# Attention and gated MLP, post-norm: normalisation scratch kept across head pairs, and four PSUM banks instead of two in the output projection

## What is computed

```python
q, k, v = x @ Wq, x @ Wk, x @ Wv                  # 16 heads of 64
s   = einsum(q, k) / 8 - 50 * strictly_upper      # per head, 2048 x 2048
att = softmax(s) @ v                              # heads joined: 1024 wide
y1  = layernorm(x + att @ Wr)
# every product below takes an int8-like row of activations and ternary weights:
#   aq(a) = clip(round(a * 127 / max|a|), -128, 127) * max|a| / 127
#   wq(w) = clip(round(w / mean|w|), -1, 1) * mean|w|
h   = silu(aq(y1) @ wq(w_gate).T) * (aq(y1) @ wq(w_up).T)
out = layernorm(y1 + aq(h) @ wq(w_down).T)
```

## Time and profile before

| | us |
|---|---|
| runs shown, median (lowest to highest) of 2 | 7385.25 (7290.29 to 7480.22) |
| the profiled execution | 7288.75 |
| its span on the slowest core (core 2) | 7287.2 |
| spans of the eight cores | 7242.9 to 7287.2 |
| attention of sequence 1 (pairs 1 to 8), from the first projection matmul | 164 to 2378 |
| attention of sequence 2 | 3961 to 5867 |
| output projection, sequence 1 and 2 | 2419 to 2607 and 5905 to 6092 |

### The profile page before, as it was taken

The page is one execution under the profiler, slowest core; times in us unless marked ns, Lnnn a source line. Parts: engine busy times, 40 slices in busy tenths (PEclk is TensorE's granted clock), DMA queues, the critical chain, the costliest instruction groups (busy, mean ns, idle before and its releaser), DMA issues.

```text
span 7287.2 us, 56300 instructions; the slowest of 8 cores (7242.9 to 7287.2 us)
## 1 busy us (share of the span) xinstructions
PE 5021.0 (69%) x17593; PEld 1861.4 (26%) x17938; DVE 2901.0 (40%) x4986; ACT 1127.3 (15%) x2132; POOL 0.2 (0%) x4
## 2 busy tenths in 40 slices
PE   0777777767778775674732877888888877576474
PEld 0222222222222232231310222222222223232131
DVE  1545455455454432321302444444444443232231
ACT  0112112112112011110100211221122211011010
POOL 0000000000000000000000000000000000000000
PEclk9888878877888888897976888998899988898887
DMA  4324233233231445445453000000000044545454
GB/s 104 93 78 105 62 105 98 65 87 107 62 87 34 134 132 145 132 150 150 133 169 71 14 18 18 12 14 18 18 16 11 10 118 127 143 131 171 129 150 141
DMA packets 803555, 649.78 MB, mean 89 GB/s; under 512 B 518336, under 2 KB 715200, under 8 KB 803264
## 3 DMA queue, kind: packets, MB, share of 16 engines
q1 hardware_dynamic: 803264, 646.16, 32.8%
HBM read 469.89 MB, written 75.50 MB: 75 GB/s over the span
## 4 chain that ended last, share of the span: by engine, by line
PE 54%; DMA 19%; DVE 15%; issue 6%; ACT 4%; SPq 1%; DVEq 0%; ACTq 0%
PE bank L160 53%; DMA wdsb<-wdT_sc 7%; ACT abuf L171 3%; DVE rls L209 3%; DMA hqT<-hq 3%; DMA XT_lo<-xlo 1%; DMA XT_hi<-xhi 1%; DMA pterT<-pter 1%; DMA pw<-Wd 1%; DVE pacc L204 1%; DVE apwl L193 1%; DVE vp L198 1%; DMA XqT<-xqtm 1%; DMA x_tm<-x 1%; PE bank L166 1%
## 5 line engine op out<-in xcount | busy, mean ns | idle before, releaser
L171 ACT ACTIVATE abuf<-bank,negC 128x512 f32<-128x512 f32 (+3 forms) x1664 | 833.3, 601 | 3061.6 <-DVE bank L188 2139.1
L160 PE MATMUL bank<-abuf,vp 128*65 128x512 f32 x2560 | 1253.9, 649 | 0.0
L160 PE MATMUL bank<-wdsb,hqT 128*128 128x512 bf16 x2008 | 539.2, 417 | 676.8 <-DMA wdsb<-wdT_sc 674.8
L160 PE MATMUL bank<-XT_hi,apwh 128*128 128x512 bf16 x1444 | 435.8, 457 | 688.2 <-DVE apwl L193 678.9
L209 DVE RECIPROCAL rls<-bank 1x512 f32<-1x512 f32 x128 | 429.4, 3355 | 705.9 <-PE bank L160 705.4
L160 PE MATMUL bank<-klp,khl 128*128 128x512 bf16 x1184 | 467.8, 395 | 325.2 <-ACT abuf L171 317.6
L160 PE MATMUL bank<-wgsb,XqT 128*128 128x512 bf16 x2010 | 493.6, 387 | 238.6 <-DMA wgsb<-wgT_sc 234.0
L160 PEld LDWEIGHTS bank<-abuf,vp 128*65 128x65 f32 x2560 | 375.8, 151 | 838.3 <-issue 838.2
L160 PE MATMUL bank<-qlo,khp 128*128 128x512 bf16 x1280 | 511.2, 399 | 27.5 <-DVE vp L198 20.0
L160 PE MATMUL bank<-wusb,XqT 128*128 128x512 bf16 x2004 | 483.2, 381 | 4.3 <-DMA wusb<-wuT_sc 2.0
L160 PEld LDWEIGHTS bank<-wdsb,hqT 128*128 128x128 bf16 x2048 | 201.4, 105 | 1013.7 <-issue 859.8
(11 more groups left out here) (90 smaller groups left out, 3346.4 us busy)
## 6 DMA issues: line engine op xcount, KB each, us to landing
wdsb<-wdT_sc SPq DMA_DIRECT2D x256, 512.0 KB, 4.0
wgsb<-wgT_sc SPq DMA_DIRECT2D x64, 1024.0 KB, 7.7
wusb<-wuT_sc SPq DMA_DIRECT2D x64, 1024.0 KB, 10.1
pw<-Wg SPq DMA_DIRECT2D x64, 512.0 KB, 4.4
pw<-Wu SPq DMA_DIRECT2D x64, 512.0 KB, 4.3
pw<-Wd SPq DMA_DIRECT2D x64, 512.0 KB, 5.0
x_tm<-x SPq DMA_DIRECT2D x8, 2048.0 KB, 18.1
xrd<-x SPq DMA_DIRECT2D x32, 512.0 KB, 5.2
```

The lines of the kernel that those rows point to most:

```text
L160: e.matmul(o, l, r, start=a, stop=b),
L171: e.activation(o, i, f, bias=b, scale=s, accum_out=a),
```

## The change

The scratch tiles of the normalisation are allocated once per sequence, in `run_seq`, and handed to `attn_pair`. The flush at the end of every pair goes; it is now called once per sequence, after the eighth pair (`flush_norm`). The closures of a pair's last block are thus called in the first block of the next pair, where before nothing was pending: `do_norm_pre`, `pump_prep(3)`, and after that block's scores `do_normalize` with `pump_prep(4)`. `avslot` is set to 1 at the head of the blocks of each pair, so a pair's eighth block always uses bank 4, which the next pair's projections into banks 0 to 3 and its transposes don't touch. In `wr_ln1` odd chunks use banks 6 and 7 instead of 4 and 5.

```diff
@@ run_seq
+            _al0 = lambda *a, **k: _es0.enter_context(self.sbg(*a, **k)).ap()
+            nbufs = (_al0("rls", [128, 512], F32),
+                     _al0("rlb", [128, 1024], BF16),
+                     _al0("osr", [64, 512], F32),
+                     _al0("onf", [64, 512], F32),
+                     [_al0("ogh0", [64, 512], BF16),
+                      _al0("ogh1", [64, 512], BF16)],
+                     [_al0("ogl0", [64, 512], BF16),
+                      _al0("ogl1", [64, 512], BF16)])
...
                     for pair in range(c.PAIRS):
-                        self.attn_pair(s, pair, XT_hi, XT_lo, wstage)
+                        self.attn_pair(s, pair, XT_hi, XT_lo, wstage, nbufs)
+                    self.flush_norm()
                     self.pump_prep(10 ** 6)
             else:
                 for pair in range(c.PAIRS):
-                    self.attn_pair(s, pair, XT_hi, XT_lo, wstage)
+                    self.attn_pair(s, pair, XT_hi, XT_lo, wstage, nbufs)
+                self.flush_norm()
+    def flush_norm(self):
+        if self.norm_pending is not None:
+            self.norm_pending[0]()
+            self.norm_pending[1]()
+            self.norm_pending = None
@@ attn_pair
-            rls = al("rls", [128, 512], F32)
...
+            rls, rlb, osr, onf, ogh, ogl = nbufs
+            self.avslot = 1
             t_ot_last = None
             for h in (0, 1):
@@ attn_pair, after the blocks
-            if self.norm_pending is not None:
-                self.norm_pending[0]()
-                self.norm_pending[1]()
-                self.norm_pending = None
@@ wr_ln1, in the matmul loop and again in the loop that empties the banks
-                            bk = 4 + jt
+                            bk = 4 + 2 * (tc % 2) + jt
```

More of the change, by code:

```diff
@@ L490, in prefetch_w, with attn_pair @@
                 src, waits=self.wsplit_toks[name])
-    def attn_pair(self, s, pair, XT_hi, XT_lo, wstage):
+    def attn_pair(self, s, pair, XT_hi, XT_lo, wstage, nbufs):
         c = self.c
```

## The result

The changed kernel is faster: the ratio to the kernel before is 0.979, 95% interval 0.973 to 0.985, so that it is not decided whether the gain is more than 2%. The profiled executions took 7149.67 (after) and 7288.75 us (before). The forecast was 7166, a ratio of 0.983. Over all runs the medians are 7333.82 (11 runs, 7114.46 to 7489.85) and 7484.58 (10 runs, 7287.15 to 7738.39); in many executions of either kernel the cores of a die, sometimes of both, were granted a lower clock and the run was some per cent longer, and the ratio is taken from the others.

What follows compares the result with a forecast made beforehand. PE, holding 54% of the span, sets the pace, so its waits count. Output projection -41, seams -53 and -46, steps +17 sum to -123, from 7288.75 to 7166 us; range 7118 to 7265.

Steps and rivals of the forecast that it cites:

- the output projection: Part 1, wr_ln1: banks 6 and 7 for odd chunks remove a 1.38 us bank wait per chunk; -41 us.
- something else takes over: Rival, also called The output projection: it is held by something else, half of the 41 us gone; 7186 us, chance 0.07.
- the seam: Between pairs, without preparation: -10.7 stop, -1.8 clock, +5.0 first block; -53 us in second sequence, -46 in first.
- the clock's 1.8 in the Q projection: Q projection after a seam: full clock without a stop before it, -1.8 us per seam in the second sequence.
- part 3: Pumped preparation steps of the first sequence: leaving the seams, partly for the first blocks, costs +17 us together.
- stops at a new weight, met elsewhere: First sequence's seams: 19 us fell where a new weight begins without its loads, and would be met elsewhere.
- The twins: A pair's fifth and sixth blocks, used to price steps in its first (+3.2 us) and second (+4.9 us).
- The first sequence gains nothing: Rival: short pumped blocks stall another 4.1 us per seam, so sequence 1's 29 us are gone; 7195 us, chance 0.14.
- Better: Rival: steps hide at seams as well as elsewhere (-17), first block gives back 3.9, not 5.0 (-15); 7134 us, chance 0.17.
- The clock: Rival: closing PE's gaps on all eight cores brings the granted clock down; 7356 us, 0.9% above before, chance 0.10.
- a clock between its levels: Sign in the profile after that would show the forecast wrong: a granted clock between the levels 1.0 and 0.5.

Runs made afterwards that it cites:

- the run with steps at the seam again: Changed kernel, no steps in a pair's first block, four at its end ahead of next weight split; first attention stage 2181 us (cores 0 to 5).

## Why the prediction was right or wrong

**Right: the output projection.** -41.0 against -41, with chunks at 10.36 for 10.37, the clock at 1.00 and the DMA share at 0.52 for 0.51. The rival that something else takes over is out.

**Right, by sums that nearly cancel: the seam.** Without steps, seven seams went from 72.3 to -1.1, 10.5 each for my 10.7; seven first blocks from 52.3 to 89.0, +5.2 each for +5.0. Of the clock's 1.8 in the Q projection less came. That projection does start at full clock, but TensorE is at half clock for longer in the rest of the pair. Windows over one pair of the second sequence, in equal parts of the pair, before and then after (columns as the earlier trace rows):

```profile
4682.30:4706.30 24.00, 22.39 (x94) 9.61 (x94) 4.20 (x7) 0.00 (x0) 0.00 (x0) 0.92 0.07 22
4706.30:4747.30 41.00, 26.95 (x105) 11.53 (x109) 24.17 (x32) 0.00 (x0) 0.00 (x0) 0.83 0.12 33
4747.30:4789.30 42.00, 34.10 (x129) 14.14 (x129) 14.76 (x48) 5.63 (x11) 0.00 (x0) 0.88 0.08 19
```

```profile
4555.80:4579.80 24.00, 20.92 (x97) 9.29 (x95) 5.65 (x9) 0.00 (x0) 0.00 (x0) 1.00 0.00 0
4579.80:4620.80 41.00, 29.00 (x109) 11.84 (x110) 22.72 (x30) 0.00 (x0) 0.00 (x0) 0.76 0.12 32
4620.80:4662.80 42.00, 33.18 (x117) 13.43 (x116) 16.91 (x51) 2.99 (x7) 0.00 (x0) 0.75 0.09 22
```

0.92 became 1.00, and 0.83 and 0.88 became 0.76 and 0.75. The third window takes in the first block, and what falls there is that block's clock. First and second block of the same pair, before and then after:

```profile
4777.02:4784.19 7.17, 7.17 (x16) 2.32 (x16) 1.20 (x4) 3.20 (x7) 0.00 (x0) 0.69 0.00 0
4784.19:4800.27 16.08, 13.63 (x35) 3.96 (x35) 7.92 (x11) 5.30 (x11) 0.00 (x0) 0.89 0.04 8
```

```profile
4650.53:4663.53 13.00, 10.28 (x19) 2.63 (x20) 7.38 (x11) 2.99 (x7) 0.00 (x0) 0.55 0.04 10
4663.53:4677.77 14.24, 11.77 (x36) 3.48 (x34) 7.91 (x11) 5.30 (x11) 0.00 (x0) 1.00 0.04 9
```

The half clock that the second block had moved into the first: 16.08 x 0.89 is 14.3, about what the second block takes now. So the projections with their transposes gained 1.2 a pair where I had booked 1.8, and the second blocks 1.2, which I had not booked. In all 7.1 a seam for my 7.5, and in the second sequence -48.4 for -53.

**Wrong: part 3, the steps; this is the step of the prediction that failed.** I had +17, it was -20, and this is what made the sum too small. By place, in the terms of part 3:

| steps of the first sequence (us) | forecast | measured |
|---|---|---|
| gone at the seams | -41 | -39.7 |
| stops at a new weight, met elsewhere | +19 | in the next row |
| first two blocks, with the stretch ahead of them | +49 | +37.5 |
| later blocks | -10 | -17.2 |
| together | +17 | -19.4 |

The seams gave up all that they had. What came back was 68 in my sum and 37.5 in the runs. Taking the 42 steps out of the first blocks again gave 36 back, which agrees. The 19 that I kept back were mostly gone: in the pairs whose seams had been long, the fourth, sixth and seventh, the steps cost 134.5 us before and 112.0 after, where the three seams had held 27.3. One stop of a new weight did move, but it had not been at a seam. PE waits for the mean of the second weight; that cost 11.2 us at the end of the fourth pair's first block before, and it stands ahead of that block's first scores after, where the stretch takes 18.7 us in place of 11.4 (core 3):

```profile
1073.57 0.19 PE L160 MATMUL bank<-pacc,ones_f 128*1 128x1 f32 x2 [0.61 <-DVE vp L198]
...
1078.94 0.55 PE L160 MATMUL bank<-ptmp,ones_row 1*128 1x1 f32 x2 [5.18 <-DVE ptmp L209]
...
1081.39 0.58 PE L160 MATMUL bank<-klp,khl 128*128 128x512 bf16 x1 [0.93 <-DVE micol_u L198]
```

The twins were not bad. For the second block I had +4.9 in six pairs, and it was 5.2 (20.3 to 51.6 in all). For the first I had +3.2, and it was 2.8 in the plain pairs; but the 11.2 us for that mean left the fourth pair's first block, so that the sum over all pairs was only 4.9. Behind all this is one mistake: I priced places by single blocks and stops and added the prices, the starts of the weights on top. The total would have been the better guide. The two attention stages differ by about 300 us for 387 steps, of which 41 stand at 28 steps of the seams. A step there costs about twice one elsewhere, and moving 28 of them should gain about 28 x (1.4 - 0.7) = 20. That is an average made after the result, and it agrees with it.

**The rivals.** *The first sequence gains nothing*: refuted, it gained 21 more than the second. *Better*: 7149.67 lies as near to its 7134 as to my 7166. Its first ground held, and more than it said: the steps cost 20 less, not merely nothing. Its second did not, the first block gave back 5.2. *The output projection*: refuted, see above. *The clock*: the output projection, the densest stage, stands at 1.00 as before. Yet a sign that I had named, a clock between its levels, is in that profile: cores 0 and 1 stood at 0.81 for 221 and 197 us of the first attention stage, cores 2 and 3 for 179 and 163 us of the last MLP stage. The profile before has none, but neither have six of the other twelve, five of them with the seams closed, and the kernel before without pumps has some. On cores 4 to 7, which had none, the mean clock is 0.858 to 0.860 against 0.859 to 0.861 before. The first attention stage on these four took 2128.6 against 2202.9, so the gain does not hang on it. Whether the change makes such stretches more or less frequent is not settled by 11 and 10 runs.

**The range.** It failed for the median of all runs, 7333.82, and the term at fault is the spread: half of the 190 us between the two runs shown stood for it, and ten runs of the kernel before spread over 451 us. That the profiled execution came within 16 us of the forecast is in part luck: the stages that I had changed gained 159 us for my 123, and 12 us of MLP, which no one forecast, went the other way. The ratio lies about at the 2% line; I gave 0.79 to within and 0.18 to beyond.

## What to carry to other kernels

Work that one engine does in order for another is best emitted where a third thing covers it: here a chain of some 10 us moved off a seam cost half of what it gained, as long as part of it landed ahead of the masks that another engine waits for, and next to nothing when it landed in a projection. Background steps have a price per place; take it as a total over a stage divided by the steps, with and without them, before pricing single blocks. And two background chains that each fit beneath a block need not fit together.

## What the runs showed of the hardware

TensorE's half clock behind a stop moved when the stop did. After the seam was closed, the granted clock in the next part of the pair shown fell from 0.83 to 0.76, although the waits on `apwl` there were the same (120.6 us over 16 before and after, the seams left out); over the seven pairs of the second sequence it fell from 0.83 or 0.84 to between 0.78 and 0.80, core by core. In the first block, where the stop did grow, it fell from 0.69 to 0.55, and in the block behind it rose from 0.89 to 1.00. A stop taken away thus gave back its own length, and of the clock's part 1.2 us in the projections and 1.2 in the second block.

Besides 1.0 and 0.5 the traces have a third level, 0.81. The output projection of the second sequence in the run with steps at the seam again, core 5 and then core 0, with the same matmuls and PE busy throughout:

```profile
5945.00:6140.00 195.00, 195.00 (x745) 80.73 (x743) 97.29 (x300) 22.94 (x46) 0.00 (x0) 0.81 0.39 106
```

```profile
5790.00:5950.00 160.00, 160.00 (x743) 72.49 (x742) 96.16 (x299) 22.94 (x46) 0.00 (x0) 1.00 0.44 129
```

The stage took 202.9 us on core 5 and 167.6 on core 0. The level came on two neighbouring cores at a time: in this run cores 4 and 5 had it in the second sequence and cores 6 and 7, of the same die, in the first. The Trainium skill ("TensorE: Matmul & The Clock Gate", Part 1) tells of a limiter that takes a whole die to 13/16 of the clock once three of its cores run dense matmuls. The level agrees, 13/16 is 0.81. The condition does not: in the profiles before and after all eight cores ran both output projections at a mean of 0.985 to 0.992, and here cores 6 and 7 ran this stage at 0.98 and 0.99 and cores 4 and 5 at 0.81. What sets it off is not shown by any run here.
